# Shift rows from 16 stationary columns, gates f and i as one 512-column piece, in a scan kernel with a gated cell behind it

## What is computed

```
mod = (silu(c) @ wmod).reshape(8, 6, 1, -1)
h = layernorm(x) * (1 + ca) + sa
x = x + ga * attn(h)                      # h_t = tanh(h_{t-1} @ A.T + x_t @ B.T); y = h_t @ C.T; out = layernorm(y + x)*gamma + beta
h = layernorm(x) * (1 + cb) + sb
# ffn(h), a scan over axis 0 of h:
ft = sigmoid(xt @ wf.T + c @ uf.T + bf)
it = sigmoid(xt @ wi.T + c @ ui.T + bi)
gt = tanh(xt @ wc.T + c @ uc.T + bc)
c  = ft * c + it * gt
x = x + gb * tanh(h @ wo.T + c_final @ uo.T + bo)
```

## Time and profile before

| | |
|---|---|
| median of 3 runs | 558.85 us (558.82 to 559.27) |
| the profiled execution | 559.37 us, of which the span from first to last instruction is 556.9 us |
| PE busy | 540.5 us, 97% of the span |
| DVE, ACT, POOL busy | 70%, 61%, 62% |
| granted TensorE clock | 0.996 of full over the span |

### The profile page before, as it was taken

How to read it: one execution, slowest core, us unless ns; L and a number is a source line. 1 busy time by engine, 2 the same in 40 slices (tenths; PEclk the granted TensorE clock), 3 DMA queues, 4 the chain that set the end, 5 groups by cost and what they waited for, 6 DMA issues and landing times.

```text
span 556.9 us, 13414 instructions
## 1 busy us (share of the span) xinstructions
PE 540.5 (97%) x4612; PEld 529.7 (95%) x4612; DVE 392.1 (70%) x910; ACT 341.2 (61%) x862; POOL 344.3 (62%) x475
## 2 busy tenths in 40 slices
PE   6999999999999999999999999999999999999994
PEld 4899999999999999999999999999999999998983
DVE  5989888785767555565766776766677676696663
ACT  3877777774566555465755566566656556667551
POOL 4767777650475444354766666677666767768453
PEclk9999999999999999999999999999999999999998
DMA  8666444425253222222233333433333333424254
GB/s 281 175 212 201 139 144 147 148 96 150 88 134 103 75 75 74 68 67 76 68 107 103 104 103 95 120 113 105 96 95 96 95 97 106 122 77 114 68 113 152
DMA packets 58514, 64.08 MB, mean 115 GB/s; under 512 B 5409, under 2 KB 49737, under 8 KB 58449
## 3 DMA queue, kind: packets, MB, share of 16 engines
q1 hardware_dynamic: 58448, 63.26, 38.3%
HBM read 46.44 MB, written 16.81 MB: 114 GB/s over the span
## 4 chain that ended last, share of the span: by engine, by line
PE 81%; POOL 6%; issue 4%; DVE 3%; ACT 3%; DMA 1%; SPq 0%; POOLq 0%; DVEq 0%; ACTq 0%
PE psOF L1590 11%; PE psI L1590 11%; PE psG L1590 11%; PE psWR L1549 7%; PE psWR L1648 6%; PE psC L1576 4%; PE psWR L1494 4%; PE psOF L1494 4%; PE psWR L1458 4%; PE psOF L1458 4%; PE psOF L1576 3%; PE psT L1627 2%; POOL wx L705 2%; PE psOF L1533 1%; PE psWR L1533 1%
## 5 line engine op out<-in xcount | busy, mean ns | idle before, releaser
L649 POOL TENSOR_TENSOR hin<-hin,uvec 128x256 f32<-128x256 f32 x64 | 51.2, 819 | 29.9 <-ACT hin L813 27.9
L656 POOL TENSOR_TENSOR hsl<-hs,hsh 128x512 fp32r<-128x512 f32 x24 | 31.0, 1290 | 49.2 <-DVE state L1313 32.6
L1294 DVE SCALAR_TENSOR_TENSOR lo<-psT,cb1T,hi 128x256 fp32r<-128x256 f32 x60 | 26.3, 479 | 41.9 <-ACT hi L878 41.9
L690 POOL TENSOR_TENSOR zn<-zn,tA 128x512 f32<-128x512 f32 x32 | 46.1, 1441 | 11.2 <-ACT zn L851 11.2
L1162 DVE TENSOR_TENSOR pre<-psWR,state 128x256 f32<-128x256 f32 x44 | 18.5, 420 | 46.3 <-PE psWR L1549 46.0
L851 ACT ACTIVATE zn<-state,nmA,rstdA 128x256 f32<-128x256 f32 x64 | 35.0, 594 | 26.1 <-POOL nmA L680 26.1
L1549 PE MATMUL psWR<-hs,AT 128*128 128x128 f32 x368 | 49.5, 274 | 0.2 <-ACT hs L837 0.2
L663 POOL TENSOR_TENSOR xin<-xin,tA 128x512 f32<-128x512 f32 x32 | 41.2, 1289 | 13.6 <-DMA tA<-rows_d 13.6
L840 ACT ACTIVATE hs<-pre 128x256 f32<-128x256 f32 x44 | 18.4, 418 | 50.6 <-DVE pre L1162 50.4
L1106 DVE SCALAR_TENSOR_TENSOR hin<-xin,mvA,uvec 128x256 f32<-128x256 f32 x56 | 39.9, 752 | 9.4 <-DMA h_park<-hin 8.9
L1549 PEld LDWEIGHTS psWR<-hs,AT 128*128 128x128 f32 x368 | 45.2, 191 | 0.4 <-ACT hs L837 0.3
(11 more groups left out here) (385 smaller groups left out, 2310.0 us busy)
## 6 DMA issues: line engine op xcount, KB each, us to landing
h_park<-hin SPq DMA_DIRECT2D x32, 256.0 KB, 2.2
hin<-h_park SPq DMA_DIRECT2D x64, 128.0 KB
xin<-in_L_attn_x_dram SPq DMA_DIRECT2D x64, 128.0 KB
tA<-rows_d SPq DMA_DIRECT2D x32, 256.0 KB, 4.4
out_dram<-state SPq DMA_DIRECT2D x64, 128.0 KB
xin<-in_L_attn_x_dram SPq DMA_DIRECT2D x28, 256.0 KB, 2.9
tW<-rows_d SPq DMA_DIRECT2D x32, 128.0 KB, 3.2
tG<-rows_d SPq DMA_DIRECT2D x24, 128.0 KB, 3.5
```

What stands on the lines that cost most here:

```text
L649: pool.tensor_tensor(h, h, sa, ALU.add).then_inc(a_h, 1)
L690: pool.tensor_tensor(two(zn[:, :]), two(zn[:, :]), both(tA[:, m % 2, 0:D]), ALU.mult).then_inc(s_zg, 1)
```

## The change

Three things are changed.

1. The high and low parts of the few columns (sb, in_c) lie side by side, 16 columns (`sbT_hl`, `c0z_hl`). One matmul with 16 stationary columns against the high weights gives hi*hi in output rows 0 to 7 and lo*hi in rows 8 to 15; a second with the 8 high columns against the low weights adds to rows 0 to 7.
2. The weights of gates f and i lie side by side (`phi`, `plo`), so that one matmul has 512 moving columns and serves both gates. Their rows are made together at the end of unit 7; the row of gate c is made in unit 8 where the row of gate i was; nothing is left where the row of gate c was.
3. ACT copies 16 rows instead of 8. The two halves are added where rows become columns: instead of six transposes there are six ordinary float32 matmuls whose moving operand is `fold`, two 8x8 identities on top of each other. DVE makes `fold` at the end of `split_tables`.

The buffers keep their sizes in sum, so that what is allocated behind them keeps its address; `fold` is allocated last.

```
-                for name, shi, slo in ((("wf", "wi", "wc")[i], sbT_hi, sbT_lo), (("uf", "ui", "uc")[i], c0z_hi, c0z_lo)):
-                    for k in range(H):
-                        for w, few in ((whi, shi), (whi, slo), (wlo, shi)):
-                            n += 1
-                            last = pe.matmul(ps, few[:, k, :], w[name][:, k, :], start=(n == 1), stop=(n == 12))
+            def shift_rows(ps, given):
+                for i, (few, high, low) in enumerate(given):
+                    for k in range(H):
+                        pe.matmul(ps[0:2 * NB], few[:, k, :, :].rearrange("p s b -> p (s b)"), high[k],
+                                  start=(i == 0 and k == 0), stop=False, skip_group_check=True)
+                    for k in range(H):
+                        last = pe.matmul(ps[0:NB], few[:, k, 0, :], low[k], start=False, stop=(i == 1 and k == H - 1),
+                                         skip_group_check=True)
                 last.then_inc(q_gb, 1)
...
             def shift_columns():
                 pe.wait_ge(q_shr, 2)
                 for i in range(3):
                     for m in range(H):
                         at = D + (i * H + m) * NB
-                        last = pe.transpose(psI[:, at:at + NB], shr[:, i, m * P:(m + 1) * P], ident[0:NB, 0:NB])
+                        last = pe.matmul(psI[:, at:at + NB], shr[:, i, m * P:(m + 1) * P], fold[:, :], start=True, stop=True)
...
                 if u == ML:
                     project(here[1])
-                    shift_row(1)
+                    shift_rows_c()
...
                     pe.wait_ge(s_tanh, 4 * AP)
-                    shift_row(0)
+                    shift_rows_fi()
                 if u == ML:
-                    shift_row(2)
                     project(here[2])
...
-                    for i, src in enumerate((psW[0:NB, :], psI[0:NB, 0:D])):
-                        act.wait_ge(q_gb, 3 + i)
+                    for i, src in enumerate((psW[0:2 * NB, :], psI[0:2 * NB, 0:D])):
+                        act.wait_ge(q_gb, 2 + i)
...
+                dve.tensor_tensor(fold[:, :], ident[0:2 * NB, 0:NB], ident[0:2 * NB, NB:2 * NB], ALU.add).then_inc(q_sbc, 1)
...
-                pe.wait_ge(q_sbc, 5)
+                pe.wait_ge(q_sbc, 6)
```

More of the change, by code:

```diff
@@ L105, in adaln_kernel @@
         uoT = sb("uoT", [P, H, D])
-        SPLIT = ["C", "wf", "wi", "wc", "uf", "ui", "uc", "wo"]
+        SPLIT = ["C", "wc", "uc", "wo"]
+        PAIRED = {"w": ("wf", "wi"), "u": ("uf", "ui")}
+        phi = {n: sb(n + "fiT_hi", [P, H, 2, D], f32r) for n in PAIRED}
+        plo = {n: sb(n + "fiT_lo", [P, H, 2, D], f32r) for n in PAIRED}
         whi = {n: sb(n + "T_hi", [P, H, D], f32r) for n in SPLIT}
         wlo = {n: sb(n + "T_lo", [P, H, D], f32r) for n in SPLIT}
+        for w, names in PAIRED.items():
+            for g, n in enumerate(names):
+                whi[n], wlo[n] = phi[w][:, :, g, :], plo[w][:, :, g, :]
         cb1T = sb("cb1T", [P, H, NB])
         sbT = sb("sbT", [P, H, NB])
-        sbT_hi = sb("sbT_hi", [P, H, NB], f32r)
-        sbT_lo = sb("sbT_lo", [P, H, NB], f32r)
+        sbT_hl = sb("sbT_hl", [P, H, 2, NB], f32r)
         bias = sb("bias", [P, 3, H])
@@ L116, in adaln_kernel @@
         c0z = sb("c0z", [P, H, NB])
-        c0z_hi = sb("c0z_hi", [P, H, NB], f32r)
-        c0z_lo = sb("c0z_lo", [P, H, NB], f32r)
+        c0z_hl = sb("c0z_hl", [P, H, 2, NB], f32r)
         state = sb("state", [P, PAIRS * W])
@@ L159, in adaln_kernel @@
         again = sb("again", [1, 1], i32)
+        fold = sb("fold", [2 * NB, NB])
         xpre = (zn[:, :], xn2[:, :], tA[:, 0, :], tA[:, 1, :])
@@ L177, in adaln_kernel @@
         rows = wx[0:NB, len(LATE):len(LATE) + 2, :].rearrange("b i (j d) -> b (i j) d", j=2)
-        shr = wx[0:NB, 0:2, :].rearrange("b i (j d) -> b (i j) d", j=2)[:, 0:3, :]
+        shr = wx[0:2 * NB, 0:2, :].rearrange("b i (j d) -> b (i j) d", j=2)[:, 0:3, :]
+        sbT_hi, sbT_lo = sbT_hl[:, :, 0, :], sbT_hl[:, :, 1, :]
+        c0z_hi, c0z_lo = c0z_hl[:, :, 0, :], c0z_hl[:, :, 1, :]
         bo_b = wx[0:NB, len(LATE) + 2, 0:D]
@@ L1028, in split_tables @@
                 dve.tensor_copy(c0z[:, :, 0], c0[:, :]).then_inc(q_sbc, 1)
[L1029 removed]
+                dve.tensor_copy(sbT_hi, sbT[:, :, :]).then_inc(q_sbc, 1)
                 dve.wait_ge(q_sbc, 1)
[L1031 removed]
+                dve.tensor_copy(c0z_hi, c0z[:, :, :]).then_inc(q_sbc, 1)
                 dve.wait_ge(q_sbc, 2)
[L1033 removed]
+                dve.tensor_tensor(sbT_lo, sbT[:, :, :], sbT_hi.bitcast(f32), ALU.subtract).then_inc(q_sbc, 1)
                 dve.wait_ge(q_sbc, 3)
[L1035 removed]
+                dve.tensor_tensor(c0z_lo, c0z[:, :, :], c0z_hi.bitcast(f32), ALU.subtract).then_inc(q_sbc, 1)
+                dve.tensor_tensor(fold[:, :], ident[0:2 * NB, 0:NB], ident[0:2 * NB, NB:2 * NB], ALU.add).then_inc(q_sbc, 1)
             def tables(i):
@@ L1671, in shift_wo, with shift_rows_fi, shift_rows_c @@
                 last.then_inc(q_gb, 1)
-            def shift_row(i):
-                ps = (psW[0:NB, 0:D], psW[0:NB, D:W], psI[0:NB, 0:D])[i]
-                n = 0
-                for name, shi, slo in ((("wf", "wi", "wc")[i], sbT_hi, sbT_lo), (("uf", "ui", "uc")[i], c0z_hi, c0z_lo)):
+            def shift_rows(ps, given):
+                for i, (few, high, low) in enumerate(given):
                     for k in range(H):
-                        for w, few in ((whi, shi), (whi, slo), (wlo, shi)):
-                            n += 1
-                            last = pe.matmul(ps, few[:, k, :], w[name][:, k, :], start=(n == 1), stop=(n == 12))
-                last.then_inc(q_gb, 1)
+                        pe.matmul(ps[0:2 * NB], few[:, k, :, :].rearrange("p s b -> p (s b)"), high[k],
[3 more added lines that the diff above has]
+                                         skip_group_check=True)
+                last.then_inc(q_gb, 1)
+            def shift_rows_fi():
+                shift_rows(psW, [(few, [phi[w][:, k, :, :].rearrange("p g d -> p (g d)") for k in range(H)], [plo[w][:, k, :, :].rearrange("p g d -> p (g d)") for k in range(H)])
+                                 for few, w in ((sbT_hl, "w"), (c0z_hl, "u"))])
+            def shift_rows_c():
+                shift_rows(psI[:, 0:D], [(few, [whi[w][:, k, :] for k in range(H)], [wlo[w][:, k, :] for k in range(H)])
+                                         for few, w in ((sbT_hl, "wc"), (c0z_hl, "uc"))])
             def shift_columns():
```

## The result

The kernel after takes **560.67 us** (median of 11 runs, 559.16 to 561.23), the kernel before on the same chip 558.73 us (median of 11, 558.17 to 559.6). The ratio is 1.0026, with a 95% interval of 1.0017 to 1.0035: slower by a quarter of a per cent. On the 558.85 us of the forecast this ratio makes 560.3; the forecast was 559.8. Of the 69 executions of the kernel before beside the experiments, 68 took 557.66 to 559.88 us at a mean clock of 0.995 to 0.998; the other took 567.03 at 0.948 and does not enter the ratios and means. The profiled execution took 560.67 us with a span of 558.9, against 559.37 and 556.9.

What follows compares the result with a forecast made beforehand. Bound: PE, 97% busy, plus a chain from `project(c2)` over DVE, POOL and ACT to `tokens(0)`. 0.39 us later there and 1.33 for the fold matmuls put step 20 0.94 later: 558.85 + 0.94 = 559.8 us, range 558.9 to 560.5.

Steps and rivals of the forecast that it cites:

- 512 columns for 0.224 us: PE's shift rows: a 512-column f32r matmul taken at 0.224 us, bounds 0.117 and 0.426; PE's list 1.47 us shorter.
- `project(c2)` 0.39 later: On PE: the pair f and i ahead of it takes 1.79 us where one row took 1.40.
- the second bound: Chain from the end of `project(c2)` over DVE, POOL and ACT's `xn` to `tokens(0)`, not shortened, starting 0.39 us later.
- The third path: DVE from `row_stats(0)` over the adds of steps 18 and 19 to step 20, which by it starts 0.2 us later.
- Twelve loads of 0.111 us: Six fold matmuls on PE ahead of step 20, two records each: 1.33 us, bounds 0.73 and 2.29.
- The 0.37 us given for the six transposes: Time taken for the old transposes ahead of step 20, 0.061 us apart, beside 1.33 for the new matmuls.
- `fold` at nothing: Small DVE instruction done by about 135.65, ahead of `shift_wo`; cover some 0.1 us, cost taken as 0.
- Behind it PE is dense until step 21 ... the 0.94 stays to the end.: Behind step 20: its 0.94 us lateness passes along PE and the chain to `tokens(2)` and the end.
- Rival 4, the clock: Idle PE ahead of step 19 and `tokens(0)` drops the clock to 1.2 GHz; about 2.4 us, 562; chance 2%.
- The late stretch: 535 to 540 us, 1.0 us idle with the clock at 1.00, cited against a fall of the clock.
- the likeliest case: Step 20 0.94 us later, kept to the end: 559.8 us, own range 559.5 to 560.0, chance 56%.
- the 30%: Whole kernel: chance of being slower by over 0.2%, summed as 20 + 2 + 8.

Runs made afterwards that it cites:

- e4_fi_late: Kernel after with the pair of rows f and i moved behind step 17, fold kept: 557.74 us, ratio 0.9982 to the kernel before.
- e6_before_order: Kernel before with only the order changed, gate i's row made behind gate f's, ahead of `project(c2)`: 559.96 us, ratio 1.0021.
- e2_transpose: Kernel after with the fold undone (six transposes of 16 rows, DVE adds the halves), pair kept: 558.6 us, ratio 0.9998 to the kernel before.
- r_after: Kernel after run once more without any edit: 559.86 us, ratio 1.0025 to the kernel before.
- e3_before_f32: Kernel before with the six transposes as ordinary float32 matmuls against the identity: 559.37 us, ratio 1.0004.
- e1_fill: Kernel after with 8 unread matmuls ahead of step 19 and 5 ahead of `tokens(0)`: 559.92 us, ratio 1.0024 to the kernel before.
- r_fill: The kernel of `e1_fill` run again in the second session: 560.0 us, ratio 1.0019 to the kernel before.
- e5_late_transpose: Kernel after with rows f and i behind step 17 and transposes of 16 rows, halves added on DVE: 557.12 us, ratio 0.9972 to the kernel before.

## Why the forecast was right, and where it failed

- **512 columns for 0.224 us.** 8 of them lie between 136.47 and 138.31: 0.230 each. Right, 0.05 us small in the sum of eight.
- **`project(c2)` 0.39 later, and the second bound with it.** Measured 0.38 at PE, 0.39 at DVE's z, 0.37 at the last statistic, `xn` and `tokens(0)` (150.32, forecast 150.34). Shown from three sides: `e4_fi_late` moves both ends 1.3 us forward, `e6_before_order` moves both back without any new work, and filling the idle time with 13 matmuls moves nothing. The list of PE is 1.4 us shorter, and that became the 0.91 and 0.51 us of idle time. These experiments show that `project(c2)` bounds `tokens(0)`; what its 0.39 us alone costs in time no run singles out, and `e2_transpose`, which has them without the fold, is level with the kernel before.
- **The third path.** Step 18's add at 147.75 (forecast 147.77), step 19's at 150.74, 0.15 later (forecast 0.19 to 0.24). Right, and it decides nothing.
- **Twelve loads of 0.111 us.** Measured 0.119, with loads of 181 to 187 ns. Right in mechanism, 0.1 us small. The 0.37 us given for the six transposes is small too: where step 20 doesn't wait, they take 0.57 (`e2_transpose`, `e6_before_order`); the sum didn't use it. The Trainium skill, "TensorE: Matmul & The Clock Gate", section "LDWEIGHTS (loading the stationary operand)", gives a load in ns as its columns divided by 1.2, 107 ns for 128, whatever the number of rows; the equal 1.43 us with 8 and with 16 rows agrees, at 119 ns. The Trainium skill's gap of about 25 ns for few moving columns (same page, "Back-to-back issue gap") would give the twelve 0.30 us. The same row, which the prediction read in part, has about 62 ns for another way of decoding: 0.74 for the twelve, and near the transposes' 61 ns. The measurement of 1.43 decides against both as the price of these twelve.
- **`fold` at nothing.** It took 0.15 us at 135.38 and nothing waited. Right.
- **"Behind it PE is dense until step 21 ... the 0.94 stays to the end."** Step 20 was 1.02 late. Where the clock didn't fall, +0.81 arrived by the mean time (559.60; forecast 559.8) and +0.95 by the mean span. About 0.2 came back between step 20 and step 21: 6.66 us before, 6.50 in `r_after`. Not forecast, and its cause is open (below).
- **Rival 4, the clock: the step that failed.** The mechanism was named and its chance was set at 2%, since 1.0 us idle late in the kernel had left the clock alone. By times and mean clocks it happened in 10 of 22 executions. It sets the first median, 560.67, which is beyond the range of 558.9 to 560.5: six of those 11 executions were in the upper group. In `r_after` only four of 11 were, and the median of 559.86 lies in the range. So on which side of the range's end a median of 11 falls is luck, and the ratio of 1.0026 too depends on the mix of the two groups, which was not forecast. Two things were wrong in the reading. The late stretch was taken as the case to compare with, but there the idle time is not followed by 1.43 us of matmuls with 8 columns; the experiments that take away either one, idle time (24 runs, and 11 of `e4_fi_late`) or fold (11 of `e2_transpose`), have no execution at 0.993 or 0.994. And the price was set at 2.4 us, for two groups of matmuls; measured is one stretch of 3.4 us at half the clock, which costs 1.5.
- **Slips in the prediction's sums.** A fifth of 56% is 11 and not the 8 that went into the 30%. And the bounds named for the likeliest case, added up, give 559.7 to 560.1 and not 559.5 to 560.0. The median forecast and the range stand without them.

So of the +2.1 us of mean in the upper part of the first measurement (560.91 against 558.79), 0.8 is the forecast's own mechanism and 1.3 the clock. That new work ahead of `project(c2)` costs is shown by `e4_fi_late` and `e6_before_order`, and that the fold costs 1.0 in the kernel after by `e2_transpose`; done alone in the kernel before, the fold's second records show in PE's rows (0.58) and are not resolved in the time. The two costs don't simply add. That it takes idle times and fold together to bring the clock down fits these 46 executions and the 11 of `e3_before_f32`, but the fall itself was seen in one profile, and one of the 11 of `e6_before_order`, which has idle times (0.40 us ahead of step 17, 0.51 ahead of `tokens(0)`) and transposes, stands alone at 560.97 with a mean clock of 0.994: it may have had one too. Why the fall comes in half of the executions with the same schedule is not settled.

## What to carry to other kernels

A shorter list on an engine that is busy for 97% is worth nothing where instructions further on wait for a chain that starts at one of its earlier results; find that result (here the end of `project(c2)`) and put nothing ahead of it that can stand behind it. Moving the new pair one step later turned a loss of 0.8 us into a gain of 1.0, and undoing the fold brought it to 1.6. A float32 matmul with few moving columns cost two full loads of its stationary operand here, 0.238 us (1.43 for six) against 0.095 for a transpose (0.57 for six). And saved time that turns into idle time on PE is not neutral: here, with thin matmuls right behind it, it went with a fall of the clock in some executions only. Such a change has to be run more than ten times and its times looked at singly, with the span beside each: a median of 11 from two groups says little.

## What the runs showed of the hardware

- **The clock can fall in the middle of a dense kernel.** After 0.91 and 0.51 us idle and 1.43 us of thin matmuls it was at half from about 152.8 to 156.2 us, though PE was busy for the whole of 3.4 us; it cost 1.4 us at once and 1.5 by the means of the two groups. Idle time alone (0.92 and 0.52 in `e2_transpose`) or thin matmuls alone (`e4_fi_late`, `e3_before_f32`) gave no sign of it in 33 executions.
- **Single profiles differ by up to 1 us ahead of the change.** The steps of `e1_fill` from 140 us on are about 0.95 later than in the first profile of the kernel after, though the two kernels' lists on PE don't differ until 147 us. At the start, the same four matmuls near 9 us last 1.03 to 1.91 us, and the records of the first ones about 2.05, with the clock column at 1.00 throughout; so the profile doesn't show that the prediction's 2.05 us of the earlier trace rows are those of a low clock.
- **The time outside the span varies too**, from 1.7 to 3.4 us, and most in the kernels with the fill.
- **The way from step 20 to step 21** took 6.66 us in the profile of before and 6.65 in `e6_before_order`, but 6.50 or 6.51 in `r_after`, `r_fill`, `e1_fill`, `e2_transpose`, `e3_before_f32`, `e4_fi_late` and `e5_late_transpose`. Even `e3_before_f32`, which changes six instructions ahead of it, has 6.51. The gates' records behind step 20 stand 0.117 us apart in the profile of before and 0.114 in `r_after`. Nothing that was run here tells why.
